# The second attention's projection, moved between the expert units of the layer before it

## The reference

```python
x = layernorm(x + softmax_attention(x))            # layer 0, attention
logits = x @ router_weight                         # layer 0, experts: 8 experts, the best two of each token
w = softmax over the top 2 logits, zero elsewhere
gu = x @ gate_up_proj + gate_up_proj_bias          # for each expert
act = (clip(up) + 1) * glu(min(gate, 7))
out = sum over e of w[:, e] * (act @ down_proj[e] + down_proj_bias[e])
x = layernorm(x + out)                             # x2, what the projection reads
q, k = x @ Wq.T, x @ Wk.T                          # layer 1, attention: 16 heads of 16 features
v = x @ Wv.T
y = causal attention with (1 + s + s*s/2) in place of exp(s), s = q.k / 4
x = layernorm(x + y @ Wo.T)
x = layernorm(x + capacity_experts(x))             # layer 1, experts
```

## Time and profile before

| | |
|---|---|
| median of 3 runs | 849.43 us (847.52 to 850.48) |
| the profiled execution's own time | 850.17 us |
| its span, first to last instruction | 848.5 us |
| busy in the span: TensorE, VectorE, ScalarE, GpSimd | 663.7, 549.5, 439.1, 409.1 us |
| mean granted clock of TensorE | 0.898 of 2.4 GHz |

### The profile page before, as it was taken

The page is one execution under the profiler, slowest core; times in us unless marked ns, Lnnn a source line. Parts: engine busy times, 40 slices in busy tenths (PEclk is TensorE's granted clock), DMA queues, the critical chain, the costliest instruction groups (busy, mean ns, idle before and its releaser), DMA issues. The chain is left out here.

```text
span 848.5 us, 18182 instructions
## 1 busy us (share of the span) xinstructions
PE 663.7 (78%) x6567; PEld 417.8 (49%) x6567; DVE 549.5 (65%) x1564; ACT 439.1 (52%) x658; POOL 409.1 (48%) x597
## 2 busy tenths in 40 slices
PE   6748999999869999999977759999996514988500
PEld 3423555555435666666654436676674203555400
DVE  6977888888558898888896653444546883222115
ACT  5433777777746555555535656676763540232102
POOL 7853777777740000000015765666664603778744
PEclk9975999999979999999998987999998755899765
DMA  4774453432000000000004789889861070354354
GB/s 159 241 228 95 114 176 108 121 85 73 5 1 1 1 1 2 1 1 1 2 0 149 243 277 212 198 181 196 190 150 36 22 204 20 73 128 99 34 91 128
DMA packets 134982, 85.79 MB, mean 101 GB/s; under 512 B 11248, under 2 KB 131568, under 8 KB 134768
## 3 DMA queue, kind: packets, MB, share of 16 engines
q1 hardware_dynamic: 128112, 79.33, 35.0%
q0 software_dynamic: 5632, 4.33, 3.6%
q10 hardware_dynamic: 1152, 0.98, 0.4%
HBM read 54.73 MB, written 29.49 MB: 99 GB/s over the span
## 5 line engine op out<-in xcount | busy, mean ns | idle before, releaser
L2164 ACT ACTIVATE a_prob<-a_ps_pair 128x1024 f32<-128x1024 f32 x96 | 93.1, 1023 | 48.0 <-PE a_ps_pair L2000 36.4
L1835 ACT ACTIVATE a_prob<-a_ps_pair 128x1024 f32<-128x1024 f32 x96 | 96.4, 1023 | 14.8 <-PE a_ps_pair L1638 12.0
L2176 POOL TENSOR_SCALAR_AFFINE_SELECT a_prob<-a_prob 128x512 f32<-128x512 f32 (+1 forms) x96 | 76.7, 807 | 51.0 <-ACT a_prob L2164 50.8
L1876 POOL TENSOR_SCALAR_AFFINE_SELECT a_prob<-a_prob 128x512 f32<-128x512 f32 (+1 forms) x96 | 75.7, 789 | 42.4 <-ACT a_prob L1835 41.8
L1774 DVE TENSOR_REDUCE a_mx<-a_ps_pair 128x4 f32<-128x1024 f32 x64 | 77.8, 1220 | 24.9 <-PE a_ps_pair L1679 23.3
L922 POOL TENSOR_SCALAR xn<-xn,stats,norm_b_rstd 128x128 f32<-128x128 f32 x8 | 6.4, 806 | 175.0 <-POOLq L411 175.0
L478 PEld LDWEIGHTS m_ps_n<-wd,m_act 128*128 128x128 f32 x512 | 66.3, 192 | 29.0 <-issue 27.4
L701 ACT ACTIVATE m_up<-m_ps_u,m_bup 128x512 f32<-128x512 f32 x64 | 44.0, 687 | 65.2 <-PE m_ps_u L466 65.2
L590 DVE SCALAR_TENSOR_TENSOR xn<-m_ps_n,m_wt,xn 128x128 f32<-128x128 f32 x256 | 71.7, 343 | 0.2 <-DVE xn L590 0.2
L478 PE MATMUL m_ps_n<-wd,m_act 128*128 128x128 f32 x512 | 67.5, 275 | 1.0 <-DVE xn L590 0.8
L466 PE MATMUL m_ps_u<-m_x1T,wgu 128*128 128x512 f32 x128 | 66.9, 605 | 0.0
(11 more groups left out here) (295 smaller groups left out, 1535.0 us busy)
## 6 DMA issues: line engine op xcount, KB each, us to landing
qst<-scratch_q SPq DMA_DIRECT2D x64, 128.0 KB, 3.0
kst<-scratch_k SPq DMA_DIRECT2D x64, 128.0 KB, 3.2
scratch_q<-p_parts SPq DMA_DIRECT2D x16, 384.0 KB, 2.4
scratch_k<-p_parts SPq DMA_DIRECT2D x16, 384.0 KB, 2.5
qst<-scratch_q SPq DMA_DIRECT2D x32, 192.0 KB, 3.1
kst<-scratch_k SPq DMA_DIRECT2D x32, 192.0 KB, 3.5
c_w<-in_w SPq DMA_DIRECT2D x8, 578.0 KB, 3.9
scratch_q<-parts SPq DMA_DIRECT2D x16, 256.0 KB, 2.5
```

Of the source, the lines that this page charges most:

```text
L1835: nc.scalar.activation(prob[:, r % 6, :], pair[(0, 2, 1)[j]][:, :], ACT.Exp, scale=scale, bias=0.0).then_inc(s_e, 1)
L1876: nc.gpsimd.affine_select(out=blk, in_=blk, compare_op=ALU.is_ge, fill=0.0, base=0, pattern=[[0, n], [1, P]], channel_multiplier=-1).then_ ...
L2164: nc.scalar.activation(prob[:, r % 6, :], pair[r % 2][:, :], ACT.Square, scale=scale, bias=1.0).then_inc(s_e, 1)
L2176: nc.gpsimd.affine_select(out=blk, in_=blk, compare_op=ALU.is_ge, fill=0.0, base=0, pattern=[[0, n], [1, P]], channel_multiplier=-1).then_ ...
```

## The change

`project_layer1` and the block around it are gone; the projection is done in `expert_layer0`.

- TensorE: from unit 8c+11 on (`next_at`), at the end of six units one after the other, comes a step for chunk c: the four transposes of `xn` (`turn_next`), four projections, v. Chunk 7 (`tail`) is done after the last unit. The routing transposes move to unit 8c+3, the bias to 8c+5, and use one PSUM buffer instead of two; the other (`ps_d`) takes the transposes, the projections and v, one at a time.
- VectorE: in unit 8c+9, right after the last accumulation of chunk c, the row statistics, their merge and the three seed steps of the root. In the units behind a projection the residual stands ahead of `clip`.
- GpSimd: the root's three turns and the shift, fourteen steps on four columns (`refine_root`), then the four `lo` of the chunk.
- ScalarE: in unit 8c+11 all four tiles are normalised (`renormalise`), then the transposes are copied; `hi`, `mid` and v's copy follow at the ends of the units.
- Chunk 7: the root is refined by VectorE, and ScalarE and VectorE normalise two tiles each.
- SP: two stores of 256 columns for each result where one of 512 was, into a scratch in DRAM that is laid out by batches of 256 tokens, where a load's rows are 4 KB long instead of 512 B; four slots are loaded ahead (`AHEAD1`) instead of two.

The diff, cut to its core:

```diff
-BUFS1, AHEAD1 = 4, 2
+BUFS1, AHEAD1 = 4, 4
+PBUFS = 4
...
-        turn_at = [E - 1] + [E * c + 2 for c in range(1, NCH)]
-        bias_at = [E + 1] + [E * c + 4 for c in range(1, NCH)]
+        turn_at = [E - 2] + [E * c + 3 for c in range(1, NCH)]
+        bias_at = [E - 1] + [E * c + 5 for c in range(1, NCH)]
+        stats_at = [E * c + E + 1 for c in range(NCH - 1)]
+        next_at = [E * c + E + 3 for c in range(NCH - 1)]
+        tail = NCH - 1
+        next_steps = {n0 + i: (c, i) for c, n0 in enumerate(next_at) for i in range(6)}
...
+            @block.sync
+            def _(sp):
+                for n in range(4 * NCH):
+                    c, i = n // 4, n % 4
+                    sp.wait_ge(s_lo, n + 1)
+                    half = P * (i % 2)
+                    for b in range(2):
+                        sp.dma_start(scratch[i // 2][2 * c + b, :, half:half + P, :].rearrange("s p t -> p s t"),
+                                     parts[:, n % PBUFS, :, T * b:T * b + T]).then_inc(s_store[n % PBUFS], 16)
+                    if 7 <= n < 7 + AHEAD1:
...
+                        load_slot(sp, n - 7, stacks, scratch, s_first)
...
+                def turn_next(c):
+                    pe.wait_ge(s_x2a, 4 * c + (4 if c < tail else 2))
+                    if c == tail:
+                        pe.wait_ge(s_x2v, 2)
...
+                    out = ps_d if c < tail else ps_r
+                    for t in range(4):
+                        last = nc.tensor.transpose(out[:, t * P:(t + 1) * P], xn[:, 4 * c + t, :], ident[:, :])
+                    last.then_inc(s_xp2, 1)
+
+                def project(n):
+                    c, i = n // 4, n % 4
+                    pe.wait_ge(s_xT2, c + 1)
+                    if c < tail:
+                        after(pe, s_r1, n if i else 0)
+                    nc.tensor.matmul(projected(n)[:, :], wqk[:, i, :], x2T[:, c % 2, :], start=True, stop=True).then_inc(s_proj, 1)
...
                     if n in bias_at:
                         add_bias(bias_at.index(n))
+                    if n in next_steps:
+                        next_layer(*next_steps[n])
                 for n in (units - 2, units - 1):
                     reduce(n)
+                for n in range(units, max(next_steps) + 1):
+                    next_layer(*next_steps[n])
+                turn_next(tail)
...
+                def seed_root(c):
+                    h = slice(4 * c, 4 * c + 4)
+                    ve.wait_ge(s_ag, c + 1)
+                    nc.vector.tensor_scalar(var2[:, h], stats[:, h, 1], EPS, None, ALU.add).then_inc(s_seed, 1)
...
+                def residual(n):
+                    ve.wait_ge(s_hi, n + 1)
+                    after(ve, s_lo, n - 1)
+                    nc.vector.tensor_tensor(resid[:, n % 2, :], projected(n)[:, :], level(n, 0), ALU.subtract).then_inc(s_r1, 1)
...
+                    if n - 1 in next_steps and 1 <= next_steps[n - 1][1] < 5:
+                        residual(4 * next_steps[n - 1][0] + next_steps[n - 1][1] - 1)
                     clip(n)
...
+                    if n in stats_at:
+                        row_stats(stats_at.index(n))
+                        seed_root(stats_at.index(n))
+                residual(4 * tail - 1)
...
+                def renormalise(c):
+                    act_e.wait_ge(s_sh2, c + 1)
+                    for t in range(4 * c, 4 * c + (4 if c < tail else 2)):
+                        nc.scalar.activation(xn[:, t, :], xn[:, t, :], ACT.Identity, scale=rstd2[:, t:t + 1],
+                                             bias=shift2[:, t:t + 1]).then_inc(s_x2a, 1)
...
+                def next_layer(c, i):
+                    if 2 <= i:
+                        mid(4 * c + i - 2)
+                    if i == 0:
+                        copy_x2(c)
+                    elif i < 5:
+                        hi(4 * c + i - 1)
+                    else:
+                        copy_v(c)
...
                         copy_weights(turn_at.index(n))
+                    if n in next_at:
+                        renormalise(next_at.index(n))
+                    if n in next_steps:
+                        next_layer(*next_steps[n])
...
+                def refine_root(c):
+                    h = slice(4 * c, 4 * c + 4)
+                    v, t, r = var2[:, h], root[:, h], rstd2[:, h]
+                    pool.wait_ge(s_seed, 3 * c + 3)
+                    for turn in range(3):
+                        step(nc.gpsimd.tensor_tensor(t, r, r, ALU.mult))
+                        step(nc.gpsimd.tensor_tensor(t, t, v, ALU.mult))
+                        step(nc.gpsimd.tensor_scalar(t, t, -0.5, 1.5, ALU.mult, ALU.add))
+                        step(nc.gpsimd.tensor_tensor(r, r, t, ALU.mult))
+                    step(nc.gpsimd.tensor_scalar(t, r, -1.0, None, ALU.mult))
+                    nc.gpsimd.tensor_tensor(shift2[:, h], t, stats[:, h, 0], ALU.mult).then_inc(s_sh2, 1)
...
                 for c in range(NCH):
...
+                    if c < tail:
+                        refine_root(c)
                     for i in range(4):
...
+                        lo(4 * c + i)
```

More of the change, by code:

```diff
@@ L457, in add_bias @@
                         here = slice(t * P, (t + 1) * P)
-                        last = nc.tensor.matmul(ps_bias[c % 2][:, here], wT[:, c % 2, here], bd[:, :], start=True, stop=True)
+                        last = nc.tensor.matmul(ps_r[:, here], wT[:, c % 2, here], bd[:, :], start=True, stop=True)
                     last.then_inc(s_bm, 1)
@@ L479, in reduce, with project_v @@
                     last.then_inc(s_dn, 1)
+                def turn_next(c):
+                    pe.wait_ge(s_x2a, 4 * c + (4 if c < tail else 2))
+                    if c == tail:
+                        pe.wait_ge(s_x2v, 2)
+                    if c == 0:
+                        pe.wait_ge(s_lk, NCH)
+                    after(pe, s_vc, c)
+                    if c == tail:
+                        pe.wait_ge(s_y, NCH)
+                    out = ps_d if c < tail else ps_r
[8 more added lines that the diff above has]
+                    nc.tensor.matmul(projected(n)[:, :], wqk[:, i, :], x2T[:, c % 2, :], start=True, stop=True).then_inc(s_proj, 1)
+                def project_v(c):
+                    pe.wait_ge(s_xT2, c + 1)
+                    if c < tail:
+                        pe.wait_ge(s_r1, 4 * c + 4)
+                    else:
+                        pe.wait_ge(s_vc, c)
+                    for t in range(4):
+                        here = slice(t * P, (t + 1) * P)
+                        last = nc.tensor.matmul(ps_d[:, here], x2T[:, c % 2, here], wv1[:, :], start=True, stop=True)
+                    last.then_inc(s_vp, 1)
+                def next_layer(c, i):
+                    if i == 0:
+                        turn_next(c)
+                    elif i < 5:
+                        project(4 * c + i - 1)
+                    else:
+                        project_v(c)
                 turn_x(0)
@@ L655, in _ @@
                         add_bias(bias_at.index(n - 1), n - 1)
[L656 to L663, removed]
+                    if n in stats_at:
+                        row_stats(stats_at.index(n))
+                        seed_root(stats_at.index(n))
+                residual(4 * tail - 1)
                 for n in (units - 2, units - 1):
                     accumulate(n)
-                row_stats(NCH - 1)
-                merge_rows(NCH - 1)
+                row_stats(tail)
+                seed_root(tail)
+                ve.wait_ge(s_seed, 3 * tail + 3)
+                finish_root(tail)
+                for i in range(4):
+                    residual(4 * tail + i)
             @block.scalar
@@ L739, in _ @@
                         copy_weights(turn_at.index(n))
+                    if n in next_at:
+                        renormalise(next_at.index(n))
+                    if n in next_steps:
+                        next_layer(*next_steps[n])
+                for n in range(units, max(next_steps) + 1):
+                    next_layer(*next_steps[n])
+                renormalise(tail)
+                copy_x2(tail)
+                hi(4 * tail)
+                for n in range(4 * tail + 1, 4 * tail + 4):
+                    hi(n)
+                    mid(n - 1)
+                copy_v(tail)
+                mid(4 * tail + 3)
             @block.gpsimd
@@ L765, in load_slot @@
[L765 to L819, removed]
@@ L820, in _, with lo @@
+                def lo(n):
+                    pool.wait_ge(s_mid, n + 1)
+                    nc.gpsimd.tensor_tensor(level(n, 2), resid[:, n % 2, :], level(n, 1), ALU.subtract).then_inc(s_lo, 1)
                 for c in range(NCH):
+                    if c < tail:
+                        refine_root(c)
                     for i in range(4):
[L822 to L825, removed]
```

228 lines of the change are left out of this document (101 added, 127 removed).

## The result

The changed kernel takes **882.8 us** (median of 4 runs, 881.9 to 883.58) where the kernel before took 849.11 beside it (4 runs, 847.52 to 850.48): a ratio of 1.0397, 95% interval 1.0376 to 1.0418. It is 33.7 us slower; the forecast was 28 slower, 877 in a range of 860 to 890. The span is 881.4 us instead of 848.5, the mean granted clock 0.884 instead of 0.898.

The account below looks back on a forecast made before the run. TensorE was taken to bound experts and attention, with the projection a 68.3 us stage between. Terms 33.4 + 29.5 + 11.9 + 21.8 = 96.6 us replace 68.3, +28.3: 877 us, range 860 to 890.

Parts of the forecast that it names:

- the steps: Forecast's terms: in the experts, projections 33.4, stalls 29.5 and clock 11.9 us; after the last expert matmul, 21.8 us.
- The moved projections: Between expert units: transposes, four projections and v add 4.77 us of TensorE a chunk, seven chunks, 33.4 us.
- The cover: In units behind a projection: other engines' added work costs nothing; without it, at most 19 us for VectorE's residuals.
- The stalls: At xn's transposes in unit 8c+11: TensorE waits six times 4.0 us and 5.5 in chunk 0, 29.5 us.
- The chain: From unit 8c+9's start: accumulate, statistics, seeds, GpSimd's steps and ScalarE's tiles take 12.25 us; TensorE arrives at 8.27.
- GpSimd's 4.19: Between seeds and ScalarE's tiles: fourteen GpSimd root steps take 4.19 us, taken from rows with 16 columns.
- The clock: Behind each of seven waits at the transposes: the clock falls to half, 1.7 us lost each, 11.9 us.
- The rival with a held clock: At the same waits: the clock does not fall, +16.4 us, 866 us; chance 0.15.
- The tail: From last expert matmul to the attention's first instruction: chunk 7's own chain takes 21.8 us, 20 to 23.5.
- The attention as long as before: Attention after the projection: its length stays unchanged; longer load rows and four slots loaded ahead gain nothing.
- The rival "covered": At the transposes: the wait is covered, no stall, 13.1 us faster, 836 us; chance 0.10 of faster.
- floor of 2.4 us: At the transposes: even if GpSimd's steps cost nothing, ScalarE's weights copy and tiles leave a 2.4 us stall.

Follow-up runs that it names:

- run 9: Changed kernel with all roots on VectorE, xn's transposes one unit later (8c+12) and ScalarE's tiles one unit earlier: 838.59 us, 0.9865 of before.
- run 1: Changed kernel with the transposes of xn two units later, at unit 8c+13: 849.4 us, 1.0009 of before.
- run 11: Changed kernel with VectorE's activate of units 9 and later taking one input from PSUM instead of SBUF: 885.51 us, 1.0416 of before.
- run 4: Changed kernel with five projections of old data, result overwritten, ahead of each wait at the transposes: 872.47 us, 1.0279 of before.
- run 3: Changed kernel with all chunks' roots refined on VectorE instead of GpSimd, transposes still at 8c+11: 862.99 us, 1.0167 of before.
- run 5: Changed kernel with all roots on VectorE and the transposes one unit later, at 8c+12: 852.43 us, 1.0034 of before.
- run 2: Changed kernel with the transposes of xn one unit later, at unit 8c+12: 853.06 us, 1.0047 of before.
- run 6: Changed kernel with the transposes at 8c+13 and v's matmuls of the first six chunks at 8c+19: 849.91 us, 1.0016 of before.

## Why the prediction was right

Direction, size and cause were right, and some 6 us were missing. From first expand to last down projection the experts took 272.6 us instead of 189.6, 83.0 more, where the steps had 74.8; the tail took 21.95 where they had 21.8. Point by point:

- *The moved projections, 33.4 us.* Right: 4.76 us in a chunk, the period of run 9 less that of before. The cover held; in the changed kernel no wait stands at a projection (run 1 shows how it can go).
- *The stalls, 29.5 us.* Mis-sized: 37.6, six times 5.0 and 7.56 in chunk 0, where 4.0 and 5.5 stood. The chain was put at 12.25 us and is 13.43. Accumulate (4.37), statistics (1.39), seeds and ScalarE's tiles (1.65 against 1.62) are as forecast; **the failed step is GpSimd's 4.19**, which is 5.25 (and 4.18 in run 11). In chunk 0 it is 5.70, and accumulate ends 0.6 us later in the chain than in the earlier trace rows. "The rows are the same instructions, also beside a busy VectorE" was wrong in its second half: VectorE was not running clip and activate there. In the last stage a step of 16 columns took 0.22; in the experts a step of 4 columns takes 0.20, but 0.7 where an activate is running. The forecast had 5.4 for the wait as its upper bound; 5.0 lies inside.
- *The clock, 11.9 us.* Right in size: seven falls, and 83.0 less 33.4 and 37.6 leaves 12.0. Run 4 and run 3 give 1.85 and 1.7 for one. By the rule of the Trainium skill that the forecast gives ("TensorE: Matmul & The Clock Gate", section on HAM oscillation) each wait pays the return again: the trace agrees, seven times in seven, and run 3's shorter waits did so five times in six. The rival with a held clock, 866, is out. But the size rests on the wait it stands behind: in run 11 it is 34.04 - 22.21 - 4.77 - 4.21 = 2.85. That 1.7, taken from a pause of 2.2 us in another stage, came so near is in part luck.
- *The tail, 20 to 23.5.* Right, 21.95, although its parts move: the clock is half for the transposes and the first projections, as counted.
- *The attention as long as before.* Wrong by 2 us, in the kernel's favour: its start had the full clock back after some 3.5 us instead of 9.6. As far as the runs show this is luck: in runs 3 and 4, with the same tail (22.1 us each), the attention took 144.6 and 144.8 us, and in the traces here it took 142.4 in four kernels and 143.8 to 144.8 in the others. The longer rows of its loads and the four slots loaded ahead show no gain, as forecast.
- *The rival "covered", 836*, is what the schedule could have been: run 9 at 838.6. The forecast's floor of 2.4 us, ScalarE's own tiles, held as long as they stood behind that unit's gate; the earlier root alone did not break it (run 5), one unit's move of the tiles did.

## What to carry to other kernels

A chain through three engines that feeds an in-order TensorE is worth nothing early if one engine's program has its part in the unit where the result is wanted: look for the unit in which each link is *issued*, and move the links one by one, since each wait hides the next. In these runs a wait of 5 us on a dense TensorE cost some 2 us of clock as well: removing it gains more than its length, filling it gains the clock's part alone (run 4), and shortening it may gain nothing (run 11). Measure small steps beside the instructions that they will really run beside.

## What was not expected of the hardware

GpSimd stands still while VectorE runs certain instructions. In the changed kernel 98 GpSimd steps refine the roots of the experts; 28 of them began while VectorE's clip or activate ran, and each of the 28 ended 0.05 to 0.10 us after that instruction ended. By line, in that kernel (count, then busy us and mean ns):

```profile
L938 POOL TENSOR_TENSOR m_root<-m_root,m_var 128x4 f32<-128x4 f32 x21 | 9.0, 428 | 1.6
L939 POOL TENSOR_SCALAR m_root<-m_root 128x4 f32<-128x4 f32 x21 | 7.3, 350 | 1.8
L937 POOL TENSOR_TENSOR m_root<-m_rstd 128x4 f32<-128x4 f32 x21 | 4.8, 231 | 57.8 <-DVE m_rstd L726 56.7
```

The same steps differ only in what runs beside them. Beside accumulate, which reads one input from PSUM, a step takes 0.20. In chunk 0 the five steps that began beside a routing instruction with two SBUF inputs ended 0.06 to 0.07 us after it; the two beside a reduce, which has one, took 0.20 and ended before it. Run 6 shows the same rule (28 of 28) with other steps hit, and run 11 takes it away by moving one input of activate to PSUM. By the Trainium skill ("SBUF — State Buffer", section "Who interferes with whom") a VectorE instruction with two SBUF inputs and a GpSimd instruction that reads SBUF share a read port that one holds for its whole length. The trace agrees for activate; clip has one SBUF input and holds GpSimd as well (14 steps of 0.31 to 0.45 us), which the page has for its two-port modes; no run here varied clip, so its reason is not shown.

Also new: a wait that was shortened by 0.8 us left the period where it was (run 11). And waits of 2.21 us were followed by the half clock in five of six chunks of run 3, while one of 2.35 us in run 2 and the six of 1.80 us in run 6 were not followed by it.
